# Two-stage convolution block: the third 3x3 convolution computed in fp32 in 64-column weight blocks instead of in three split products

## The reference

```python
x = x + _L0_conv_ref(_gn(x), ...)      # (8, 32, 64, 64) fp32, per-channel normalization first
x = x + _L1_conv_ref(_gn(x), w1, w2, w3)

def _L0_conv_ref(x, ...):              # 4 groups of position-dependent 3x3 weights
    mu = softmax(gate)                 # 1x1 convolution of x, over 4 groups
    v = einsum('bchw,dc->bdhw', x, value_w)
    kern = exp(-(pu / sig_u) ** 2 - (ps / sig_s) ** 2)   # pu, ps, sig from a 1x1 convolution of x
    w = mu * kern;  w = w / (sum(w over groups and taps) + 1e-6)
    agg = einsum('brsl,bcsl->brcl', w, patches_3x3(v))
    return einsum('bkhw,ok->bohw', agg, pw_w) + pw_b

def _L1_conv_ref(x, w1, w2, w3):       # 3x3, padding 1, NCHW
    x = conv3x3(x, w1)                 # 32 -> 64 channels
    x = conv3x3(x, w2)                 # 64 -> 64
    return conv3x3(x, w3)              # 64 -> 32
```

## Time and profile before

| | before |
|---|---|
| median of 3 runs | 541.21 us (540.34 to 541.48) |
| the profiled execution | 541.46 us, of which the span is 539.6 us |
| PE busy | 470.1 us (87%) |
| DVE busy | 419.2 us (78%) |
| ACT, POOL busy | 207.2 us (38%), 199.9 us (37%) |
| mean granted TensorE clock | 0.970 |

### The profile page before, as it was taken

One profiled execution on the slowest core, in us unless ns is written; L12 is line 12 of the kernel. 1 busy time (PEld: TensorE's weight loads), 2 busy tenths in 40 slices (PEclk: granted clock), 3 DMA queues, 4 the chain that ended last, 5 costly groups with the idle time before them and its releaser, 6 DMA issues.

```text
span 539.6 us, 6937 instructions
## 1 busy us (share of the span) xinstructions
PE 470.1 (87%) x2498; PEld 386.1 (72%) x2498; DVE 419.2 (78%) x553; ACT 207.2 (38%) x386; POOL 199.9 (37%) x95
## 2 busy tenths in 40 slices
PE   1249563899898999899999999999979999999995
PEld 1238353766786788678886897878767878787894
DVE  2799998889998998978898989898988989221211
ACT  3522412374156434372428314751537324341110
POOL 2164347801682175208470359027540613000000
PEclk9999795699999999999999999999999999999999
DMA  5100002600117100731072014501361035108201
GB/s 151 39 4 1 0 27 54 145 19 1 40 36 172 38 28 17 160 73 47 4 162 67 13 40 110 112 22 40 76 137 33 0 79 130 33 1 183 57 0 39
DMA packets 38225, 32.21 MB, mean 60 GB/s; under 512 B 24112, under 2 KB 28720, under 8 KB 38192
## 3 DMA queue, kind: packets, MB, share of 16 engines
q1 hardware_dynamic: 38192, 31.77, 24.7%
HBM read 5.66 MB, written 4.19 MB: 18 GB/s over the span
## 4 chain that ended last, share of the span: by engine, by line
PE 55%; DVE 22%; ACT 7%; issue 7%; POOL 3%; SPq 3%; DMA 2%; DVEq 0%; ACTq 0%; POOLq 0%
PE conv_ps L407 41%; DVE prod L1116 9%; PE val_ps L458 4%; PE agg_ps L473 4%; SPq L277 2%; DVE prod L1126 2%; PE conv_ps L421 2%; PE pw_ps L488 2%; POOL gn L1888 2%; PE geo_ps L440 2%; DMA xq<-y 2%; ACT L1542 1%; ACT c_lo L1595 1%; DVE y L1159 1%; DVE st L950 1%
## 5 line engine op out<-in xcount | busy, mean ns | idle before, releaser
L1116 DVE TENSOR_TENSOR prod<-val_ps,tapw 128x2048 f32<-128x2048 f32 x80 | 180.5, 2283 | 9.8 <-PE val_ps L458 8.5
L1902 POOL TENSOR_TENSOR prod<-prod 128x2048 f32<-128x2048 f32 x23 | 108.3, 4711 | 173.3 <-DVE prod L1116 173.3
L407 PE MATMUL conv_ps<-c_hi,wc_hi 128*128 128x448 f32 (+2 forms) x384 | 152.3, 397 | 1.1 <-ACT c_lo L1595 1.1
L407 PE MATMUL conv_ps<-c_hi,wc_lo 128*128 128x448 f32 (+2 forms) x384 | 144.3, 376 | 0.0
L407 PE MATMUL conv_ps<-c_lo,wc_hi 128*128 128x448 f32 (+2 forms) x384 | 144.2, 375 | 0.0
L407 PEld LDWEIGHTS conv_ps<-c_hi,wc_hi 128*128 128x128 f32 x384 | 72.6, 189 | 15.6 <-issue 5.0
L1918 POOL TENSOR_TENSOR xs<-xn 128x1024 f32<-128x1024 f32 x32 | 72.5, 2275 | 29.2 <-PE val_ps L458 17.0
L1126 DVE TENSOR_TENSOR prod<-prod 128x2048 f32<-128x2048 f32 x35 | 81.7, 2336 | 0.4 <-issue 0.2
L407 PEld LDWEIGHTS conv_ps<-c_hi,wc_lo 128*128 128x128 f32 x384 | 72.3, 188 | 10.4
L407 PEld LDWEIGHTS conv_ps<-c_lo,wc_hi 128*128 128x128 f32 x384 | 72.7, 189 | 8.1
L1587 ACT ACTIVATE c_hi<-conv_ps 128x512 fp32r<-128x512 f32 (+4 forms) x88 | 41.5, 484 | 87.5 <-PE conv_ps L407 87.0
(11 more groups left out here) (106 smaller groups left out, 440.6 us busy)
## 6 DMA issues: line engine op xcount, KB each, us to landing
xq<-y SPq DMA_DIRECT2D x128, 132.0 KB, 2.6
xraw<-in_x SPq DMA_DIRECT2D x32, 128.0 KB, 2.7
x2r<-x SPq DMA_DIRECT2D x128, 32.0 KB, 1.9
out_y<-x2r SPq DMA_DIRECT2D x32, 128.0 KB, 2.8
prod<-in_w SPq DMA_DIRECT2D x1, 576.0 KB, 5.2
xn<-xn SPq DMA_DIRECT2D x16, 24.8 KB, 1.8
prod<-in_w SPq DMA_DIRECT2D x1, 384.0 KB, 3.5
prod<-in_w SPq DMA_DIRECT2D x1, 192.0 KB, 2.5
```

Source lines behind the costliest of these rows:

```text
L407: mm = nc.tensor.matmul(bank[:, 0:conv_cols(n)], weights, lo if part == 1 else hi, start=term == part == 0, stop=final and part == 2)
L1116: v.tensor_tensor(dst, val.unsqueeze(2).to_broadcast([P, B, R, C]), wgt.unsqueeze(3).to_broadcast([P, B, R, C]), ALU.mult).then_inc(mult_d ...
L1902: p.tensor_tensor(product(i, TAPS * h + a), product(i, TAPS * h + a), product(i, TAPS * h + b), ALU.add).then_inc(add_g, 1)
```

## The change

1. The third convolution uses plain fp32 operands. Its weights `w3_sb` are loaded as they are; its input is one tile `c2`, written once by ACT from the second convolution's banks. `c2_hi`, `c2_lo`, `take_high` and `low_part` of chunks 4 to 8 go away (N_SPLIT, the number of chunks that are split, falls from 9 to 4; N_MID is the new name for 9).
2. The 9 terms of 3 matmuls become 6 terms of 2 matmuls. Each has a weight block of 64 columns (two output rows) and writes one half of the PSUM partitions; the blocks that are zero are left out (`TILES`).
3. Chunks 9 and 10 wait for high parts instead of low parts.
4. `w_stage`, `wc_hi` and `wc_lo` hold 9 blocks instead of 18.
5. The order of all engines' calls is written anew. On SP `by_quads(0)` now comes after the four `by_slots(0, ...)`, and `store(2)` and `store(4)` before the last `by_slots` of images 3 and 5.

```diff
-TERMS = {1: 3, 2: 6, 3: 9}
+TERMS = {1: 3, 2: 6, 3: 6}
+TILES = (((0, 1), (1, 1)), ((0, 0), (1, 2)))
-N_SPLIT = 9
+N_SPLIT, N_MID = 4, 9
...
-        NC = (3 + 6 + 9) * P
+        NC = (3 + 6) * P
+        w3_sb = sb("w3_sb", [P, 9 * P])
...
-        w_stage = prod[:, 4:6, :].rearrange("p n f -> p (n f)")[:, 0:NC]
+        w_stage = prod[:, 4, 0:NC]
...
-        c2_hi = sb("c2_hi", [P, H // 2 + 1, PW], F32R)
-        c2_lo = sb("c2_lo", [P, H // 2 + 1, PW], F32R)
+        c2 = sb("c2", [P, H // 2 + 1, PW])
...
+                        elif pn < N_MID:
+                            pe.wait_ge(hi_done, N_MID * pj + pn + 1)
...
+                    elif n < N_MID:
+                        wait_lows(pe, j, lo_needed(n))
                     else:
-                        wait_lows(pe, j, lo_needed(n))
+                        pe.wait_ge(hi_done, N_MID * j + (7 if n == N_MID else 9))
...
+                else:
+                    _layer, j0, m = CHUNKS[n]
+                    dx = term // 2
+                    for rows, t in TILES[term % 2]:
+                        at = (3 * t + dx) * P + MID * rows
+                        src = c2[:, 2 * j0 + t:2 * (j0 + m - 1) + t + 1:2, dx:dx + W]
+                        mm = nc.tensor.matmul(bank[MID * rows:MID * rows + MID, :], w3_sb[:, at:at + MID], src,
+                                              start=term == 0, stop=final)
...
             def take_high(j, n):
-                if n in LOW_V[j]:
+                if n in LOW_V[j] or n >= N_SPLIT:
                     return
...
             def low_part(j, n):
-                if n in LOW_V[j]:
+                if n in LOW_V[j] or n >= N_SPLIT:
                     return
...
-            by_quads(0)
             halo(2)
             by_slots(0, 0)
             by_slots(0, 1)
             by_slots(0, 2)
             by_slots(0, 3)
+            by_quads(0)
...
             by_slots(3, 2)
+            store(2)
             by_slots(3, 3)
-            store(2)
             by_quads(3)
```

The third convolution's 12 terms of an image in PE's new order (of 54 now: numbers 42 to 53), with other work of PE between the stretches; image 0 as the example:

```diff
+            convs(0, 40, 43)
             transpose_sums(2, 0)
+            convs(0, 43, 45)
+            transpose_sums(2, 1)
             values(2, 8)
+            convs(0, 45, 50)
             values(2, 9)
             convs(0, 50, 51)
+            transpose_sums(2, 2)
+            convs(0, 51, 54)
```

More of the change, by code:

```diff
@@ L342, in _ @@
             by_slots(5, 2)
+            store(4)
             by_slots(5, 3)
-            store(4)
             by_quads(5)
@@ L402, in conv_term @@
                         pe.wait_ge(pads_p, N_PADS_P)
-                w, hi, lo = conv_operands(n, term)
                 final = term == TERMS[CHUNKS[n][0]] - 1
-                for part in range(3):
-                    weights = (wc_lo if part == 2 else wc_hi)[:, w * P:(w + 1) * P]
-                    mm = nc.tensor.matmul(bank[:, 0:conv_cols(n)], weights, lo if part == 1 else hi,
-                                          start=term == part == 0, stop=final and part == 2)
+                if n < N_MID:
+                    w, hi, lo = conv_operands(n, term)
+                    for part in range(3):
+                        weights = (wc_lo if part == 2 else wc_hi)[:, w * P:(w + 1) * P]
+                        mm = nc.tensor.matmul(bank[:, 0:conv_cols(n)], weights, lo if part == 1 else hi,
+                                              start=term == part == 0, stop=final and part == 2)
+                else:
+                    _layer, j0, m = CHUNKS[n]
[5 more added lines that the diff above has]
+                                              start=term == 0, stop=final)
                 if final:
@@ L555, in _ @@
             gn2_sums(0, 0)
-            values(1, 6)
             gn1_sums(2, 0)
@@ L639, in _ @@
+            convs(1, 12, 19)
+            transpose_sums(2, 5)
+            convs(1, 19, 21)
             values(3, 2)
-            transpose_sums(2, 5)
-            take_high(1, 3)
-            convs(1, 20, 23)
+            transpose_sums(2, 6)
             values(3, 3)
+            convs(1, 21, 23)
+            values(3, 4)
             convs(1, 23, 24)
-            transpose_sums(2, 6)
+            transpose_sums(2, 7)
             convs(1, 24, 26)
-            values(3, 4)
-            transpose_sums(2, 7)
@@ L662, in _ @@
+            convs(1, 39, 42)
+            gn1_sums(4, 0)
             gn2_sums(2, 0)
-            convs(1, 40, 45)
-            gn1_sums(4, 0)
-            take_high(1, 7)
+            gn1_sums(4, 1)
+            convs(1, 42, 43)
             gn2_sums(2, 1)
-            values(3, 9)
-            gn1_sums(4, 1)
-            take_high(1, 8)
-            convs(1, 45, 53)
+            convs(1, 43, 46)
+            geometry(4)
             transpose_sums(3, 0)
-            convs(1, 53, 54)
-            geometry(4)
+            convs(1, 46, 54)
@@ L747, in _ @@
-            transpose_sums(4, 4)
-            convs(3, 13, 14)
-            take_high(3, 2)
-            convs(3, 14, 16)
-            transpose_sums(4, 5)
-            convs(3, 16, 21)
-            transpose_sums(4, 6)
-            convs(3, 21, 23)
+            convs(3, 7, 10)
+            take_high(3, 2)
+            convs(3, 10, 12)
+            pointwise(4, 0)
+            convs(3, 12, 17)
+            transpose_sums(4, 4)
+            transpose_sums(4, 5)
+            convs(3, 17, 18)
+            transpose_sums(4, 6)
@@ L802, in _ @@
+            convs(4, 3, 5)
+            take_high(4, 0)
+            convs(4, 5, 6)
+            values(6, 0)
+            convs(4, 6, 8)
             take_high(4, 1)
-            convs(4, 8, 15)
+            convs(4, 8, 11)
+            pointwise(5, 0)
+            convs(4, 11, 12)
             values(6, 1)
-            convs(4, 15, 17)
+            convs(4, 12, 15)
+            transpose_sums(5, 4)
             take_high(4, 2)
-            convs(4, 17, 19)
-            pointwise(5, 0)
-            convs(4, 19, 20)
+            convs(4, 15, 21)
@@ L837, in _ @@
+            values(6, 6)
             gn2_sums(5, 1)
[L838 to L841 removed]
+            convs(4, 43, 50)
+            values(6, 7)
             geometry(7)
+            convs(4, 50, 51)
+            values(6, 8)
+            convs(4, 51, 53)
             transpose_sums(6, 0)
[L844 to L846 removed]
+            convs(4, 53, 54)
             transpose_sums(6, 1)
[L848 removed]
@@ L872, in _ @@
+            transpose_sums(6, 5)
             convs(5, 24, 26)
-            transpose_sums(6, 5)
-            convs(5, 26, 29)
-            take_high(5, 5)
+            values(7, 1)
+            convs(5, 26, 27)
+            transpose_sums(6, 6)
+            convs(5, 27, 28)
+            values(7, 2)
+            convs(5, 28, 29)
+            transpose_sums(6, 7)
             convs(5, 29, 31)
-            values(7, 2)
-            convs(5, 31, 32)
-            take_high(5, 6)
             values(7, 3)
-            transpose_sums(6, 6)
@@ L1252, in _ @@
             mult(2, 3)
+            mult(2, 4)
             gn2_stats(1, 0)
-            mult(2, 4)
             gn1_stats(3)
@@ L1379, in _ @@
             mult(5, 7)
+            result(3, 0)
             mult(5, 8)
-            result(3, 0)
             mult(5, 9)
@@ L1429, in _ @@
             tap_weights(7, 5)
+            residual(6, 0)
             tap_weights(7, 6)
@@ L1443, in _ @@
             gn2_bias(6)
+            add_products(7, 0, 2)
+            split_low(6)
+            add_products(7, 0, 3)
             mult(7, 5)
-            split_low(6)
-            add_products(7, 0, 2)
+            mult(7, 6)
             result(5, 0)
-            mult(7, 6)
-            add_products(7, 0, 3)
+            result(5, 1)
             mult(7, 7)
             mult(7, 8)
-            result(5, 1)
+            mult(7, 9)
             add_products(7, 1, 1)
             add_products(7, 1, 2)
-            mult(7, 9)
             add_products(7, 1, 3)
             residual(7, 0)
+            residual(7, 1)
             gn2_stats(7, 0)
-            residual(7, 1)
             gn2_stats(7, 1)
```

725 lines of the change are left out of this document (303 added, 422 removed).

## The result

The changed kernel took 535.17 and 530.98 us in the runs that the ratio rests on, against 541.35 us (540.34 to 541.49) for the kernel before on the same chip: ratio 0.9851 (95% interval 0.9818 to 0.9884), that is 8 us or 1.5% faster. Its two longer runs (539.21 and 542.88 us), with granted clocks of 0.949 and 0.944 against 0.961 and 0.965, are left out of that ratio; with all four the median is 537.19 us, which is 4 us or 0.8% faster. Part 4 of the explanation comes back to the spread.

The account below looks back on a forecast made before the run. PE and DVE, both nearly full, with a chain after `split_low(6)`, were taken as bounds; 9.9 before it, 0.5 and 1.65 made 12.1 us off 541.46, 529.4, then 529.1 at the median, put at 528.5; range 522 to 533.

Parts of the forecast that it names:

- the gain is eaten by DVE and the chains: Rival: DVE's dependency waits before `split_low(6)` stay; some 538 us, or 534 with half the shed time arriving; 20%.
- The round: New third convolution: one round of 512 fp32 columns costs 0.46 us, 24 rounds or 11.04 us per image.
- the pairing: New third convolution: a term's two 64-column matmuls run side by side; the rival that this fails: 584 us, 9%.
- additional round: Rival: halves issued matmul by matmul give each third-convolution stretch one round more, 8.2 us in all; 537 us, 7%.
- The switch: Changing block widths around each stretch of the new third convolution: 0.27 us per stretch, 5.7 us in images 0 to 4.
- The last third convolution: Image 7's third convolution, alone on PE at the end: 1.65 us gained.
- 9.9 us shed before `split_low(6)`, 0.8 of it arrives: PE in images 0 to 5: cheaper third convolution and fewer `take_high`, less switching; 7.9 us of gain counted.
- The granted clock unchanged: Sign for the changed profile: the whole kernel's granted clock stays as before.
- The weight split: DVE before its first `mult`: 2.55 us become 1.3, of which 1.0 us was counted as gain.
- The low-part waits: PE waits less for low parts once 35 on ACT and 5 on DVE go: 1.0 us, between 0 and 6.
- 57 us behind `split_low(6)`, fixed but for 0.5: From `split_low(6)` to image 7's convolutions: transfers and normalization, of which only 0.5 us is gained.
- the order at nothing: New call order on all engines: no gain or cost, up to 2 us per moved store if cover fails.

Follow-up runs that it names:

- experiment 2: Changed kernel with four of six terms of the third convolution left out in images 0 to 5; 544.17 us, ratio 1.0059 to the kernel before.
- each filling: Kernels with thrown-away matmuls added to keep PE busy, on the changed kernel or the one before; from 539.73 to 558.42 us.
- experiment 11: Changed kernel with 13 thrown-away matmuls in two places where PE waits, before `transpose_sums(1, 0)` and image 0's first convolution; 539.73 us, ratio 0.9956.
- experiment 1: Changed kernel's new third convolution with every engine's calls in the order of the kernel before; 545.33 us, ratio 1.0065.
- experiments 4: Changed kernel with `store(2)` and `store(4)` behind the last `by_slots` of images 3 and 5 again; 539.21 us, ratio 0.9953.
- experiment 12: Changed kernel with slot 3 transfers issued first on own semaphores, so chunk 0 waits for five transfers instead of eight; 528.66 us, ratio 0.9765.
- experiment 3: Changed kernel with two of ten DVE multiplications of images 1 to 6 doing only half their columns; 539.41 us, ratio 0.996.

## Why the prediction was right in its number and wrong in its way

The measured ratio on 541.2 us gives 533.1 us: inside the range, on the predicted side, 4.6 us above the forecast. By the median of all four runs it would be 537.2, 8.7 above. It lies at the edge of the rival "the gain is eaten by DVE and the chains" (534 to 538), or inside it. By its mechanism that rival is the one that came true, with the chain, and to a part the clock, as what ate, and not DVE's load. That the number fell into the range was luck in part: the sum's largest term didn't come, and terms priced too low made up for some of it.

1. **The round (0.46 predicted, 0.43 measured)** and the pairing were right. 24 rounds took some 10.4 us in image 7, not 11.04. The Trainium skill, "TensorE: Matmul & The Clock Gate" (What overlaps and what doesn't), says that matmuls start and end in strict order. The trace agrees in the way that the prediction read it: the first halves of both blocks start together, the second halves 0.43 us later, and there is no additional round.
2. **The switch (0.27 per stretch)** was too dear. In image 7 the first matmul starts at 516.84, where the last step of 384 columns (0.18) would have ended at 516.75, and the first round takes 0.06 more: 0.15 us in all. The last third convolution therefore gave 2.6 us up to `result` and not 1.65.
3. **The step that failed: "9.9 us shed before `split_low(6)`, 0.8 of it arrives".** PE did shed it (10.3 us less busy between 60 and 438), the convolution's matmuls with minus identity fell to 28 as predicted, and on balance none of it arrived: `split_low(6)` at 437.30, not near 427. I had taken the share of busy time over 378 us (PE 92%, DVE 90%) as a measure of what arrives. It is a mean over two legs with different limits, one where PE is at 99% and one where it waits for a chain; the saving lay in the second. The trace of before had the row to see it: PE already waited 1.86 us for input at 224.97, after 5.11 us of work in 6.90, and the earlier trace rows had such waits at 4.2 us. I read them as small. They should have been read as the sign that PE's work just before them is free; after the change they are 8.8 us, and 19.1 in experiment 2. The legs say the same with the order held: 7.8 us less PE work in five legs B, and the legs 0.7 us longer. What the new order gave in leg B (5.2 us over five images), leg A took back, an estimated 3.4 of it by the clock.
4. **"The granted clock unchanged"** was wrong: 0.961 against 0.970, and from run to run 0.944 to 0.965. Of the low stretches in mid-kernel (3.4 us each at 144, 226 and 400) two lie at PE waits for input, of 3.55 us until 225.06 and 1.35 until 400.28; ahead of the one at 144 PE had waited 2.14 us until 141.04, for DVE's part of a normalization. One such stretch costs PE some 1.7 us at the head of leg A, where PE is the bound. Before had no low stretch from 104.6 us to its end. That a longer wait costs clock is argued from these places and from experiment 2 (0.903), not isolated: each filling had delays of its own. And the length of one wait doesn't settle it: in experiment 11 PE waited 3.62 us before image 2 (until 228.15) and the clock stayed up, while in experiment 1 it fell at waits of 1.89 us (until 225.16) and 1.87 us (until 451.81). Why experiment 1 is slower than before is argued in the same way: its legs A lost an estimated 4.6 us to the clock. The spread belongs to the kernel: its near copies of experiments 4 and 11 ran from 535.31 to 542.61 us and from 536.37 to 544.73, around 539. So the 8 us of the first section, from two runs, are rather too much than too little.
5. **The two terms ahead of the loop didn't arrive either.** The weight split fell from 2.55 to 1.30 us, as priced, and the first `by_slots` stands at 97.24 instead of 97.28. The low-part waits (1.0) left no trace in 280.0 against 279.4 us.
6. **"57 us behind `split_low(6)`, fixed but for 0.5"** was wrong to the good side: 52.5 us. 3.8 of it lie ahead of image 7's input, and all kernels in the new order have this but for a little (43.1 to 45.1 us where PE has no extra work, against 47.0 and 47.7 in the old). I had priced the order at nothing, as it contains the same calls. By experiment 1 the whole order is worth some 8 us to the new convolution (545.3 against 537.2, the medians of all runs). The new order with the old convolution wasn't tried, nor experiment 12's edit on the kernel before.
7. **DVE's busy time** was to stay within 4 us and fell by 8.9; nothing was gained by it, and a further relief gained nothing either (experiment 3).

So errors of both signs met. Of the predicted 12.1 us the 9.9 ahead of `split_low(6)` didn't come; 3.8 came between the inputs of images 6 and 7 where I had 0.5, and 2.4 behind image 7's input (54.0 us before, 51.6 after) where I had 1.65. 3.8 + 2.4 are the 6.2 us between the spans.

## What to carry to other kernels

Before a saving on the busiest engine is counted, find out in which leg of the period it lies: where the engine ends the leg waiting for something, its work there is free, and making it cheaper only makes the wait longer. A short wait for a transfer (1.9 us here) in an engine that is 92% busy is worth more than its length, since it marks the chain to shorten: waiting for the five transfers that are read instead of eight gave 8 us, some 3 of them through the clock, a convolution made 2.4 us cheaper per image none in the same stretch. And the converse doesn't hold: work added to such a leg costs nearly in full (4.5 of 5.4 us per image here) once the slack is used up.

When calls are moved as well, compare the legs with the order held fixed. Here the order made leg B shorter by as much as leg A grew, and the span alone showed neither.

## What the runs showed of the hardware

- Two fp32 matmuls of 128x64 weights and 512 columns, to different halves of the PSUM partitions, appear as two records each (384 for 192 matmuls). The first halves run side by side in 0.43 us, then the second halves: 0.87 us for both matmuls. In a row of matmuls to the same half each takes the 0.87 alone; issued six by six, the two blocks overlap only in part (16.0 us against 10.6 for 24).
- A load of 128x64 weights took 0.13 to 0.14 us in the rows shown, one of 128x128 0.19 us, and neither stood bare in a row of matmuls: the rounds stayed 0.43 us apart, the one-pass matmuls of 512 columns 0.24.
- After a PE wait of 3.55 us in a stretch at 2.4 GHz, the clock was granted at 1.2 GHz for 3.4 us; after the wait of 1.86 us at the same place in the kernel before it was not, and neither was it after one of 3.62 us there in experiment 11. In experiment 1 it fell at one of 1.89 us. So what makes it fall isn't the length of that wait alone; the rule is open.
